# Graph network on one core: fifty edge tiles for each destination block in place of fifty-two

## Time and profile before

| what | value |
|---|---|
| runs | 11371.26, 11374.06, 11385.44 us; median 11374.06 |
| span of the profiled execution | 11359.5 us, 14.6 us below the median |
| instructions in the profile | 328,525 |
| busy in that span | TensorE 8833.8, its weight loads 7171.9, VectorE 8475.3, ScalarE 4619.4, GpSimd 1650.1 us |
| granted TensorE clock, mean | 0.843 of full speed |

### The profile page before, as it was taken

How to read it: one execution, slowest core, us unless ns; L and a number is a source line. 1 busy time by engine, 2 the same in 40 slices (tenths; PEclk the granted TensorE clock), 3 DMA queues, 4 the chain that set the end, 5 groups by cost and what they waited for, 6 DMA issues and landing times. The chain is left out here.

```text
span 11359.5 us, 328525 instructions
## 1 busy us (share of the span) xinstructions
PE 8833.8 (78%) x100906; PEld 7171.9 (63%) x101103; DVE 8475.3 (75%) x17219; ACT 4619.4 (41%) x9076; POOL 1650.1 (15%) x2115
## 2 busy tenths in 40 slices
PE   6144667886888755899994888799899959949997
PEld 5132224664777644899994656433899956649996
DVE  7498777777999866666666666666788877788887
ACT  0021001113666411555653333477677746613333
POOL 0010000110000000566661000000000003301110
PEclk9855555555999855999997999899999979979998
DMA  1100000000444311333333999777455510000000
GB/s 38 13 0 11 4 4 8 11 11 28 166 164 165 123 36 31 121 124 121 125 124 105 324 320 321 237 248 250 130 144 143 146 55 5 5 3 3 3 3 13
DMA packets 617098, 1103.82 MB, mean 97 GB/s; under 512 B 119654, under 2 KB 207566, under 8 KB 617019
## 3 DMA queue, kind: packets, MB, share of 16 engines
q1 hardware_dynamic: 487514, 923.22, 25.6%
q10 hardware_dynamic: 121152, 168.86, 4.0%
q0 software_dynamic: 8352, 10.85, 0.4%
HBM read 901.57 MB, written 201.10 MB: 97 GB/s over the span
## 5 line engine op out<-in xcount | busy, mean ns | idle before, releaser
L2433 POOL TENSOR_TENSOR acc<-acc,m_sum 128x544 f32<-128x544 f32 (+1 forms) x637 | 810.8, 1273 | 1222.9 <-ACT m_sum L2400 946.0
L2363 PE MATMUL m_sps<-m_msg,m_oh 128*128 128x136 f32 x5096 | 722.4, 286 | 0.0
L2298 DVE TENSOR_TENSOR m_msg<-m_vps,m_msg 128x512 f32<-128x512 f32 x637 | 440.7, 692 | 365.5 <-PE m_vps L2339 290.5
L2753 PE MATMUL u_sps<-u_r,u_oh 128*128 128x128 f32 x5096 | 677.8, 276 | 27.4 <-ACT u_r L2711 27.4
L2552 DVE BATCH_NORM_STATS2 stats<-t_es 128x512 f32 x637 | 442.3, 694 | 340.8 <-ACT t_es L2585 339.6
L2737 PE MATMUL u_zps<-fcs,u_a 128*128 128x128 f32 x5112 | 676.9, 276 | 6.9 <-ACT u_a L2705 6.9
L2638 PE MATMUL g_z<-g_a,fcT 128*128 128x512 f32 x1274 | 612.7, 615 | 63.5 <-ACT g_a L2627 52.9
L1419 PE MATMUL sp_out_x<-x,sp_adj_x 128*128 128x128 f32 x4802 | 661.5, 281 | 0.0
L1432 ACT COPY sp_adj_x<-sp_aps_x 128x512 f32<-128x512 f32 x637 | 373.4, 586 | 700.5 <-PE sp_aps_x L1403 700.5
L1403 PE MATMUL sp_aps_x<-sp_ohw_x,sp_oh_x 128*128 128x128 bf16 x7644 | 545.2, 219 | 144.8 <-DVE sp_ohw_x L1370 144.8
L2564 PE MATMUL t_eps<-t_oht,p_parts 128*128 128x512 bf16 x1715 | 482.4, 384 | 220.6 <-DVE t_oht L1483 204.0
(11 more groups left out here) (587 smaller groups left out, 21401.1 us busy)
## 6 DMA issues: line engine op xcount, KB each, us to landing
u_e<-e_tiles SPq DMA_DIRECT2D x640, 256.0 KB, 2.8
e_tiles<-t_es ACTq DMA_DIRECT2D x637, 256.0 KB, 5.4
g_e<-e_tiles SPq DMA_DIRECT2D x637, 256.0 KB, 3.5
s_rows<-bucket_rows SPq DMA_DIRECT2D x148, 768.0 KB, 4.0
m_rows<-bucket_rows SPq DMA_DIRECT2D x148, 768.0 KB, 4.1
t_rows<-bucket_rows SPq DMA_DIRECT2D x148, 768.0 KB, 7.0
s_rows<-bucket_rows SPq DMA_DIRECT2D x49, 1024.0 KB, 5.3
m_rows<-bucket_rows SPq DMA_DIRECT2D x49, 1024.0 KB, 5.3
```

Of the source, the lines that this page charges most:

```text
L2363: last = nc.tensor.matmul(sps[x][:, at:at + M], oh[x][:, j * P:(j + 1) * P], msg[x][:, j * M:(j + 1) * M], start=True, stop=True)
L2433: nc.gpsimd.tensor_tensor(at, at, sums[x][:, 0:n * M], ALU.add).then_inc(added, 1)
L2753: last = nc.tensor.matmul(sps[:, :], oh[x][:, j * P:(j + 1) * P], zr[x][:, j * D:(j + 1) * D], start=(q == 0 and j == 0), stop=(q == last_ ...
```

## The change

A window gets one overflow tile, `AT` = 50 tiles that are worked on in place of 52. Sets stay 13, and `NT` = 52 stays the layout of a stored window; the thirteenth set holds two tiles (`B.held(12)` = 2), and every instruction of it works on two. The lists as they leave the fill stage are stored in 250 columns in place of 260 (500 bytes a partition). The compare of the sparse products is written anew, so that it can take one pair of tiles or two.

```diff
-        self.NT = -(-(s.NB + 3) // 4) * 4
-        self.NQ = self.NT // 4
-        self.OV = self.NT - s.NB
+        self.OV = 1
+        self.AT = s.NB + self.OV
+        self.NQ = -(-self.AT // G)
+        self.NT = self.NQ * G
...
-        self.cols = FIELDS * self.NT
+        self.cols, self.raw_cols = FIELDS * self.NT, FIELDS * self.AT
...
+    def held(self, q):
+
+        return min(G, self.AT - q * G)
...
-def pair_one_hot(nc, k, out, lst, at):
-
-    return pair_hot(nc, out[:, :], k["iota1_2"], P, lst[:, bass.ds(at, 8)], 4)
+def pair_one_hot(nc, k, out, lst, at, pairs):
+
+    return nc.vector.tensor_tensor(
+        out[:, :].rearrange("p (e q v t) -> p e q v t", e=2, q=2, t=2)[:, :, 0:pairs],
+        k["iota1_2"][:, :].rearrange("p (v t) -> p v t", t=2).unsqueeze(1).unsqueeze(1).broadcast_to([P, 2, pairs, P, 2]),
+        lst[:, bass.ds(at, 8)].rearrange("p (e q t) -> p e q t", e=2, t=2)[:, :, 0:pairs].unsqueeze(3).broadcast_to([P, 2, pairs, P, 2]),
+        ALU.is_equal)
...
     a, b = B.pieces[n]
+    end = min(b * GE, B.AT * P)
...
-                            for j in range(G):
+                            for j in range(B.held(q)):
...
-                        elif q in (5, 7, 9):
+                        elif q in (5, 7, 9)[0:OV]:
                             vs.append(over_of(b, len(vs)))
...
-                        act.dma_start(e_tiles[bass.ds(w * P, P), q * GE:(q + 1) * GE], es[x][:, :]).then_inc(stored[x], 16)
+                        act.dma_start(e_tiles[bass.ds(w * P, P), q * GE:q * GE + m], es[x][:, 0:m]).then_inc(stored[x], 16)
```

More of the change, by code:

```diff
@@ L1418, in _ @@
                                     over[:, (tile - s.NB) * width:(tile - s.NB + 1) * width]
-                                last = nc.tensor.matmul(out[:, :], adj[r][:, t * P:(t + 1) * P], rhs, start=(tile == 0), stop=(tile == NT - 1))
+                                last = nc.tensor.matmul(out[:, :], adj[r][:, t * P:(t + 1) * P], rhs, start=(tile == 0), stop=(tile == AT - 1))
                             last.then_inc(used[r], 1)
@@ L2562, in _ @@
                             pe.wait_ge(over_set, w + 1)
+                        n = B.held(q)
                         for c in range(3):
-                            nc.tensor.matmul(eps[x][:, :], PP[:, bass.ds(w * TW + c * D, D)], oht[r][:, GE:], start=(c == 0), stop=False)
-                        for j in range(G):
+                            nc.tensor.matmul(eps[x][:, 0:n * P], PP[:, bass.ds(w * TW + c * D, D)], oht[r][:, GE:GE + n * P], start=(c == 0), stop=False)
+                        for j in range(n):
                             t = q * G + j
@@ L2751, in _ @@
                             pe.wait_ge(copied, w + 1)
-                        for j in range(G):
+                        for j in range(B.held(q)):
                             last = nc.tensor.matmul(sps[:, :], oh[x][:, j * P:(j + 1) * P], zr[x][:, j * D:(j + 1) * D],
-                                                    start=(q == 0 and j == 0), stop=(q == last_q and j == G - 1))
+                                                    start=(q == 0 and j == 0), stop=(q == last_q and j == B.held(q) - 1))
                         last.then_inc(summed[x], 1)
```

151 lines of the change are left out of this document (84 added, 67 removed).

## The result

The changed kernel takes 11179.5 us (median of 4 runs, 11176.2 to 11189.5) against 11377.0 before (4 runs): ratio 0.9832, 95% interval 0.9818 to 0.9846. That is 197.5 us less, where 318.5 were forecast; 11179.5 lies 9.5 us above the range. The span of the profiled execution went from 11359.5 to 11174.6, 184.9 us less. The kernel got faster, as forecast, but by 0.62 of the forecast, and in three stages the sign was wrong too.

The account below looks back on a forecast made before the run. Each stage was given its own bound: VectorE in bf, TensorE in m, u, spg and g, DMA in t, chains in bs and x. Terms summed to 318.5 us off 11374, giving 11055 us, range 10990 to 11170.

Parts of the forecast that it names:

- The tables, bf, s, m, u and spg: Savings forecast for the tables and five stages, in this order: 5.5, 13, 20, 49, 43 and 27 us.
- the stage is one chain of a window: In x: two updates and six matmuls fewer shorten each window by 1.13 us, 55 us in all, bounds 45 and 62.
- bytes shrink by 2/52 and the stage is bound by them: In t: the byte share is 40 us, of which 34 was taken, bounds 15 and 42.
- two near limits, both of them shrinking: In g: ScalarE's waits for loads and TensorE 0.91 busy; share 26 us, 22 taken, bounds 12 and 28.
- the term, 0.35 us a window: In spx: only set 12's shorter adjacency is on the turn's path; 17 us in all, bounds 10 and 43.
- the sign of danger that the prediction named: In spx: the forecast would be wrong if the wait of some 0.6 us grew at every turn by the set's loss.
- more than all is worth: Lower granted clock where turns get longer against work: a stage of u's size would lose more than the whole gain; chance 0.02.
- the compare `bs_lt` gives 0.27: In bs: set 12's half compare saves 0.27 us of 0.68 a window; 33 us in all, bounds 25 and 41.
- The turns eat it: Rival, every stage: the last set hides behind stage-to-stage latency, so half is saved, 159 us, 11215 us; chance 0.13.
- The case for the forecast: All stages but four have an engine or DMA at 0.9 or more, so each saves near its share; chance 0.80.
- The slower compare: Rival, sparse products: the rewritten compare runs one column at a time, +0.53 us, kernel 11472 us; chance 0.04.
- a dearer store: In bf: the narrower 500-byte store was costed at nothing, its landing covered by a window; uncovered, 83 us.

Follow-up runs that it names:

- Experiments 1: The changed kernel with the mask's transfer in x issued ahead of those of the scores and ends: 11187.7 us, x 598.1 us.
- 2: The changed kernel with x's scores and mask loaded once the previous scores are turned, only the ends waiting for set 12: 11120.4 us, x 545.0.
- 10: The kernel before the change with early loads in x, six slots in t and g, and a fifth slot in spx: 11000.6 us.
- Experiment 3: The changed kernel with the thirteenth set left out of g altogether: 11184.8 us in a single run, g 681.8 us.
- 4: The changed kernel with six ring slots in place of four in t and g: 10846.0 us, t 844.9 and g 525.3.
- 5: The kernel before the change with six ring slots in place of four in t and g: 11070.0 us, t 860.1 and g 546.7.
- experiment 6: The changed kernel with six extra identity matmuls on TensorE at the end of each window of spx: 11156.6 us, spx 1106.6.

## Why the prediction was wrong

The tables, bf, s, m, u and spg came as they were worked out: 155.9 us measured, 157.5 forecast. There the step from instruction times to a stage's length was sound. The range missed because lower bounds were made from the prices of instructions, while in four stages the question was whether the instruction counted at all; each of those stages ended below its lower bound, and so did bs.

- **x, the largest miss (48 us).** The step that failed is "the stage is one chain of a window": it was so for the window before the change, with the mask's transfer running beside it. The prediction reads the DMA waits of t and g, and none in x. The earlier trace rows show the window's turn without the issue of the mask; the prediction never asked when it lands (3.97 us later, with the scan at 3.99). Experiments 1, 2 and 10 settle it: with early loads the kernel before gains nothing (596.3 for 596.0), and the changed one 43.6 us. The term itself was sized rightly: 51.0 us once the mask was out of the way.
- **t (37 us) and g (23 us).** The step that failed is "bytes shrink by 2/52 and the stage is bound by them", and "two near limits, both of them shrinking". A DMA share of 0.92 and TensorE at 0.91 were read as bounds. The waits of the earlier trace rows were for landings in a ring of four slots, and the slot of set 12 lies outside the ring's three rounds. Experiment 3 shows that set 12 is worth nothing in g, 4 and 5 that the rings set the pace in both. For g the size was right (21.4 and 19.8 us with six slots, 22 forecast). For t it was not: with six slots the half set is worth 15.2 and 12.5 us in place of 34, and why so little is open. The last 3 us by which t got longer are not settled either; its clock column fell from 0.99 to 0.97.
- **spx (19 us).** The mechanism and the size of the term, 0.35 us a window, were right, and so was the sign of danger that the prediction named: the wait at every turn grew by 0.45 us. What failed is its neighbour: of the clock I wrote that a fall would cost "more than all is worth" in a stage like u and gave it 0.02. It came as short falls in every fourth window, cost about what the term gave, and experiment 6 gets both back by adding work. The Trainium skill, "TensorE: Matmul & The Clock Gate", Part 1, says that the throttled state is the default and activity releases it; the rows agree in direction, and show that a stage in which TensorE is busy for over 0.9 of the time (1036 of 1130 us) can still fall at its turns.
- **bs (12 us).** The mis-sized term: 0.42 us a window in place of 0.68. The part that failed is "the compare `bs_lt` gives 0.27": 0.25 of it went into the ranks' wait behind the placing of set 10, and one-hot, placing and ranks make 0.14 + 0.21 + 0.07 = 0.42. This is read from one turn of the timeline and was not tried.
- **The rivals.** "The turns eat it" forecast 11215 and was nearer than the forecast in number, and that is luck: it took half from every stage. Measured, the tables and five stages gave their terms within bounds, and four stages next to nothing. Its idea, a last set hidden behind something, was nearer the truth in those four. The case for the forecast, that "all stages but bs, s, x and spx" have an engine or the DMA at 0.9 or more, was misread for bf, whose VectorE is busy 606 of 770 us; its term came all the same. The slower compare did not come: `sp_oh_x` takes 678 ns at the median where it took 680. Neither did a dearer store: bf gained its 12.1 us. Both hold by the profile of the change itself.

## What to carry to other kernels

Before a saving is multiplied by the number of windows, name for each stage what the freed time runs into next: a transfer issued at the window's end, a ring whose turns don't include the set that shrinks, or a wait that grows until TensorE's clock falls. A busy share of 0.9 doesn't prove a bound. (Landing time + work of a slot) x (uses of a slot in a window), set against the window's length, points at a ring: in t (5.4 + 0.59) x 3 = 18.0 of 21.2 us, in g (3.4 + 0.8) x 3 = 12.6 of 13.7. With six slots it is 13.4 of 17.3 and 9.4 of 10.7, so the ratio alone doesn't settle it, and the test is one more slot. Where a change falls short, remove what it ran into in both kernels and compare again: here that turned 197 us into 307, and the fixes themselves were worth 485.

## What was not expected of the hardware

- In spx the granted clock fell from 1.00 to 0.50 for some 3 us at every fourth window once the wait at the turn had grown from 0.60 to 1.05 us, the 0.87 behind it being as before; six matmuls (0.50 us) in that wait left 0.72 of it and kept the column at 1.00.
- In bs the clock column read 0.50 in one profile and 1.00 in another of the same code, with the same durations; a column like that has to be checked against the durations of matmuls.
- The DMA engines at a share of 0.90 moved 309 GB/s, 378 GB/s at 1.01 and 386 at 1.02, with landings only 0.7 to 0.8 us later. A 128 KB load landed after 3.3 us and one of 256 KB after 3.4, so a half transfer frees its slot hardly earlier.
- Where a register chose the place of a matmul's result in PSUM, a sparse product took 10 to 15 us more; the cause is open.
